# Second layer of a two-layer model in fp32r: expert weights brought to the rows by DMA through DRAM instead of by matmuls

## The chip, the cores and the metric

The kernel runs on one core of a Trainium2 chip. The metric is the device time of one execution in microseconds.

## What is computed

Input x has 4 sequences of 512 rows and 512 columns. Two layers follow each other; in both, x becomes x + s * silu(f), with s and f computed from the normalised rows.

```python
# layer 1: s = masked linear, f = FFN over the argmax of each block of 32
# layer 2:
qkv = xn @ Wqkv + bqkv
attn = softmax(q @ k.T / sqrt(128)); s = (attn @ v) @ Wo + bo
base_out = xn @ base_w.T + base_b
res_hidden = xn @ A.T                      # 64 columns
logits = xn @ router_w.T                   # 16 experts
topw, topi = top_k(softmax(logits), 2); topw /= sum(topw) + 1e-6
combine = sum(one_hot(topi) * topw)        # [row, expert]
delta = einsum('bse,bsr,eor->bso', combine, res_hidden, B)
f = base_out + delta * 0.5
```

The last product is computed as one matrix product over 16 x 64 = 1024 values per row: `prod[e*64 + r, row] = combine[row, e] * res_hidden[row, r]`, eight tiles of 128 partitions.

## The kernel before, in words

Every fp32 product is made of three fp32r matmuls: each operand is split into a rounded part (`_hi`) and the remainder (`_lo`), and `three` (L414) issues hi x hi, hi x lo and lo x hi. ScalarE rounds, VectorE or GpSimd subtract. The five engines run lists that are written out by hand in program order (`chunk` in each engine's block) and are tied together by semaphores; nothing reorders them. Layer 1 (until about 408 us) is not touched by the change but for small things. Between the layers the rows go through DRAM (`mid_state`).

Layer 2 works on one sequence at a time, here called a chunk (0 to 3); chunk 0 is written out, 1 and 2 are a loop, 3 is written out. In TensorE's `chunk` (L1368) the order is: res_hidden and logits (bank `pj[0]`), q, k and v with the transposes of the logits and of the routing weights (`comb`) between them, scores of row tile 0, then scores 1 to 3 with base products (`base`, L1324) and spreading matmuls between them, the transposes of the probabilities (`probs_transpose`, L1350), half of the products with B (`lora`, L1332), the product with v ("pv"), the other halves of lora, the output projections (`project`, L1362), then base and lora of row tiles 2 and 3, with the transposes of the next chunk's normalised rows (`transpose_rows`, L344) around lora of tile 3.

The routing weights of a row must reach all 64 partitions of each expert. Before, the transposed weights lie in `combT` (16 rows, and their remainders in 16 more), and a matmul with the 0/1 matrix `pick`, built once on GpSimd (L620 to L628), spreads them over 128 partitions:

```python
nc.tensor.matmul(pj[kt % 2][:], pick[:, kt, :], combT[:], start=True, stop=True).then_inc(spread_done, 1)
```

This is done for each of the eight tiles kt (`spread`, L1316). VectorE multiplies the bank by `res` (`prods`, L1063), ScalarE rounds the product (`prods_hi`, L799), GpSimd forms the remainder (L672), and lora waits for it (`prod_split`). The product buffer `prod` has three places, so product kt waits for remainder kt - 3.

VectorE's `chunk` (L1119) also holds the maxima of the scores (`score_peak`), the remainders of the transposed probabilities (`probs_lo`, L1070), the bias of y and s and the silu (`y_out`, `s_out`, `silu`), and for the next chunk the statistics, the normalisation (`rows_norm`, L384) and the remainders of its transposed rows (`rows_lo`, L358). The transpose of next rows 2 waits for `xT_done` of next rows 0, as both use one bank. GpSimd gates: after silu it multiplies g by s and adds x_res (`gate`, L391). Of layer 1's last four gates, the second and later ones wait for the second `qk_lo` of chunk 0 (L657).

SyncE issues all DMAs. It ends layer 1 with the four row stores of the last sequence, each after its gate, and the wait for them (L533); in layer 2 (L548) each chunk loads x_res, then x_tile of the next chunk, stores four row tiles, and waits for these stores.

Of the eight banks, `pj` are 0 and 1, `y` 2 and 3, `sc` 4 and 5, `tr` 6 and 7.

## Time and profile before

| what | value |
|---|---|
| median of 3 runs | 650.04 us (650.01 to 650.18) |
| the profiled execution, its own time | 650.05 us |
| its span in the profile | 648.2 us |
| TensorE matmuls busy | 632.3 us, 98% of the span |
| VectorE busy | 446.3 us, 69% |
| GpSimd busy | 240.0 us, 37% |
| ScalarE busy | 213.4 us, 33% |

The span runs from the first to the last instruction of the profiled execution; its own time is 1.85 us longer. Matmuls overlap in the records (one of 512 columns is listed with 0.39 us but the next starts 0.227 us after it), so a stretch is priced by its start and end, not by the sum of its records. Layer 2 begins with the matmul at 407.96 us; the chunks begin some 58.9 us apart.

### The profile page before, as it was taken

The page shows a single profiled execution, that of the slowest core. Times are in us where ns is not written, and L with a number is a line of the kernel's source. Part 1 is how long each engine was busy: PE and PEld are TensorE (multiplying, and loading weights), DVE is VectorE, ACT ScalarE, POOL GpSimd, SP SyncE. Part 2 cuts the span into 40 slices and gives each one's busy share as a digit, 9 for nine tenths or more (in the row PEclk, how much of TensorE's full clock was granted, in tenths as well). Part 3 has the DMA queues.
Part 4 walks back from the last instruction along what each step waited for, and adds up shares of the span by engine and source line. Part 5 has one row for each costly group of instructions (what it writes and reads, how often), then busy time and mean ns, then how long its engine had stood idle before and what let it go on. Part 6 is the DMA issues. An engine that isn't in the chain of part 4 may idle for free.

```text
span 648.2 us, 8466 instructions
## 1 busy us (share of the span) xinstructions
PE 632.3 (98%) x2942; PEld 509.9 (79%) x2942; DVE 446.3 (69%) x716; ACT 213.4 (33%) x379; POOL 240.0 (37%) x188
## 2 busy tenths in 40 slices
PE   7999999999999999999999999999999999999997
PEld 3768787878888878888878787778878878887887
DVE  7987776787765777765777886655765857575633
ACT  3533333312223312223322243651255035314510
POOL 2355545650000740000742644582425433351441
PEclk9999999999999999999999999999999999999999
DMA  9940000022400022300153622050140013012000
GB/s 282 400 158 1 2 0 1 26 81 52 127 17 9 26 81 70 108 16 8 32 141 95 173 82 73 17 178 1 49 147 1 16 50 129 0 41 89 2 32 33
DMA packets 42575, 46.16 MB, mean 71 GB/s; under 512 B 25072, under 2 KB 25456, under 8 KB 41904
## 3 DMA queue, kind: packets, MB, share of 16 engines
q1 hardware_dynamic: 42544, 45.76, 22.1%
q8 instruction: 18, 0.29, 0.2%
q14 instruction: 13, 0.11, 0.1%
HBM read 31.85 MB, written 8.39 MB: 62 GB/s over the span
## 4 chain that ended last, share of the span: by engine, by line
PE 81%; DVE 12%; issue 3%; ACT 1%; POOL 1%; DMA 1%; DVEq 0%; POOLq 0%; ACTq 0%; SPq 0%
PE bank L418 73%; DVE counts L940 3%; PE bank L348 2%; DVE seg_top L926 2%; DVE eq L928 2%; PE bank L1205 1%; PE bank L1359 1%; DMA first<-counts 1%; PE bank L1183 1%; DVE h_lo L970 1%; PE bank L1322 1%; DVE h L961 1%; POOL g_tile L394 1%; PE bank L1224 1%; DVE ws_raw L994 0%
## 5 line engine op out<-in xcount | busy, mean ns | idle before, releaser
L418 PE MATMUL bank<-w_hi_t,h_hi 128*128 128x512 f32 x224 | 90.4, 404 | 0.7 <-DVE h_lo L970 0.4
L761 ACT ACTIVATE h_hi<-h 128x512 fp32r<-128x512 f32 x56 | 35.4, 633 | 162.9 <-DVE h L961 162.9
L418 PE MATMUL bank<-w_lo_t,h_hi 128*128 128x512 f32 x224 | 87.6, 391 | 0.0
L418 PE MATMUL bank<-xT_hi,w_hi_t 128*128 128x512 f32 x224 | 87.4, 390 | 0.1
L418 PE MATMUL bank<-w_hi_t,h_lo 128*128 128x512 f32 x224 | 87.4, 390 | 0.0
L418 PE MATMUL bank<-xT_hi,w_lo_t 128*128 128x512 f32 x224 | 87.2, 389 | 0.0
L418 PE MATMUL bank<-xT_lo,w_hi_t 128*128 128x512 f32 x224 | 87.1, 389 | 0.0
L940 DVE TENSOR_TENSOR_SCAN counts<-restart,eq 128x512 bf16<-128x512 bf16 (+1 forms) x56 | 76.0, 1357 | 2.4
L394 POOL TENSOR_TENSOR g_tile<-g_tile,s_tile 128x512 f32<-128x512 f32 x31 | 44.3, 1430 | 88.3 <-DVE g_tile L983 44.2
L926 DVE TENSOR_REDUCE seg_top<-bank 128x16 f32<-128x512 f32 (+1 forms) x64 | 39.5, 617 | 46.2 <-PE bank L1205 46.2
L672 POOL TENSOR_TENSOR prod_lo<-prod,prod_hi 128x512 fp32r<-128x512 f32 x32 | 40.6, 1291 | 57.9 <-ACT prod_hi L801 57.8
L970 DVE TENSOR_TENSOR h_lo<-h,h_hi 128x512 fp32r<-128x512 f32 x56 | 42.0, 751 | 27.0 <-ACT h_hi L761 25.4
L380 POOL TENSOR_TENSOR rstd<-mean_var,eps 128x4 f32<-128x4 f32 x8 | 1.6, 201 | 159.1 <-DVE mean_var L374 159.1
L740 ACT ACTIVATE h<-bank 128x512 f32<-128x512 f32 x56 | 33.5, 598 | 57.4 <-DVE h_lo L970 47.3
L418 PE MATMUL bank<-b_hi,prod_hi 128*128 128x512 f32 (+1 forms) x136 | 52.1, 383 | 0.0
L418 PE MATMUL bank<-b_hi,prod_lo 128*128 128x512 f32 (+1 forms) x136 | 51.3, 377 | 0.0
L418 PE MATMUL bank<-b_lo,prod_hi 128*128 128x512 f32 (+1 forms) x136 | 51.3, 377 | 0.0
L418 PEld LDWEIGHTS bank<-w_hi_t,h_hi 128*128 128x128 f32 x224 | 42.1, 188 | 10.7 <-DVE h_lo L970 2.3
L418 PEld LDWEIGHTS bank<-w_hi_t,h_lo 128*128 128x128 f32 x224 | 42.1, 188 | 9.4
L418 PEld LDWEIGHTS bank<-xT_hi,w_hi_t 128*128 128x128 f32 x224 | 42.0, 188 | 9.1 <-ACT s_tile L695 0.4
L418 PEld LDWEIGHTS bank<-xT_hi,w_lo_t 128*128 128x128 f32 x224 | 42.0, 188 | 8.7
L418 PEld LDWEIGHTS bank<-xT_lo,w_hi_t 128*128 128x128 f32 x224 | 42.1, 188 | 8.7
(191 smaller groups left out, 1300.5 us busy)
## 6 DMA issues: line engine op xcount, KB each, us to landing
w_raw<-in_w SPq DMA_DIRECT2D x28, 256.0 KB, 10.1
x_res<-in_x SPq DMA_DIRECT2D x4, 1024.0 KB, 8.5
mid_state<-g_tile SPq DMA_DIRECT2D x16, 256.0 KB, 2.1
x_tile<-mid_state SPq DMA_DIRECT2D x4, 1024.0 KB, 7.4
x_res<-mid_state SPq DMA_DIRECT2D x4, 1024.0 KB, 5.5
out<-g_tile SPq DMA_DIRECT2D x15, 256.0 KB, 2.0
x_tile<-in_x SPq DMA_DIRECT2D x3, 1024.0 KB, 5.6
b_raw<-in_lora_b SPq DMA_DIRECT2D x2, 1024.0 KB, 5.1
```

Of the source, the lines that this page charges most:

```text
L348: last = nc.tensor.transpose(rows_bank(g, tt)[:, k * P:(k + 1) * P], x_tile[:, tt, k * P:(k + 1) * P], ident[:])
L394: nc.gpsimd.tensor_tensor(g_tile[:, tt, :], g_tile[:, tt, :], s_tile[:, tt, :], ALU.mult).then_inc(s_free, 1)
L418: last = nc.tensor.matmul(dst, a, b, start=(start and n == 0), stop=(stop and n == len(mms) - 1))
L672: nc.gpsimd.tensor_tensor(prod_lo[:, kt, :], prod[:, kt % 3, :], prod_hi[:, kt, :].bitcast(F32), ALU.subtract).then_inc(prod_split, 1)
L740: nc.scalar.activation(h[:], up[it % 2][:], ACT.Relu).then_inc(relu_done, 1)
L761: nc.scalar.activation(h_hi[:, it % 2, :], h[:], ACT.Copy).then_inc(h_hi_done, 1)
L926: nc.vector.reduce_max(seg_top[:, 0:segs], got, AX.X).then_inc(seg_max, 1)
L928: nc.vector.tensor_tensor(eq[:, 0:PW[p]].rearrange("p (s n) -> p s n", n=SEG), got, seg_top[:, 0:segs, None].to_broadcast([P, segs, SEG]), ...
L940: nc.vector.tensor_tensor_scan(kept[:, tt, 0:PW[p]], restart[:, 0:PW[p]], eq[:, 0:PW[p]], 0.0, ALU.mult, ALU.add).then_inc(sel_count, 1)
L961: nc.vector.scalar_tensor_tensor(h[:], which, 1.0, h[:], ALU.is_equal, ALU.mult).then_inc(h_masked, 1)
L970: nc.vector.tensor_tensor(h_lo[:, it % 2, :], h[:], h_hi[:, it % 2, :].bitcast(F32), ALU.subtract).then_inc(h_split, 1)
L1183: last = nc.tensor.matmul(sel[:], c1_stack[:, k, :], x[:, k, :], start=(k == 0 and x is xT_hi), stop=(k == KD - 1 and x is xT_lo))
```

## The change

The `pick` matrix and the spreading matmuls are gone. ScalarE copies the 16 transposed rows of weights to `combT` (now plain fp32, no remainder), SyncE stores them to DRAM (`expert_weights`, 32 KB), waits for the store, and copies them back with eight DMAs, each of which repeats rows over 64 partitions for two tiles (256 KB). The copies land in `spread`, which shares its place with prod_lo. These nine DMAs stand ahead of the load of x_res. VectorE multiplies `spread` by `res`, both in SBUF.

As banks 0 and 1 are free of spreading, y has four banks (0 to 3), and base of tiles 0 to 2 (and of 3, but in the last chunk) goes ahead of lora. lora waits tile by tile of prod. VectorE takes all score maxima first and the products after them: three before the remainders of the probabilities 0 and 1, the fourth between, four behind. `comb` is written once, without the padding.

```diff
@@ -172,9 +171,10 @@
+        spread = raw_at("spread", [P, KE, S], next_1l.end)
...
-        combT = next_1l.take("combT", [P, S], F32R)
+        combT = next_1l.take("combT", [P, S])
@@ -437,10 +435,12 @@
-        y = [banks[2], banks[3]]
+        y = [banks[tt] for tt in range(TT)]
+        y_end = [banks[3], banks[1]]
+        KG = KE // 4
...
-        NROUTE = 19
+        NROUTE = 18
@@ -547,6 +547,13 @@
+                sp.wait_ge(comb_out, c + 1)
+                sp.dma_start(weights, combT[0:E, :]).then_inc(st_weights, 16)
+                sp.wait_ge(st_weights, c * 16 + 16)
+                for i in range(4):
+                    for j in range(EPT):
+                        sp.dma_start(spread[j * R:(j + 1) * R, i * KG:(i + 1) * KG, :],
+                                     weights_of[j:j + 1, i * KG:(i + 1) * KG, :].to_broadcast([R, KG, S])).then_inc(ld_spread[i], 16)
@@ -820,7 +818,7 @@
-                        nc.scalar.activation(combT[0:2 * Q, :], tr[0][0:2 * Q, :], ACT.Copy).then_inc(comb_hi, 1)
+                        nc.scalar.activation(combT[0:E, :], tr[0][0:E, :], ACT.Copy).then_inc(comb_out, 1)
@@ -829,21 +827,17 @@
-                prods_hi(c, 0)
-                prods_hi(c, 1)
-                probs_exp(c, 1)
-                prods_hi(c, 2)
-                prods_hi(c, 3)
-                probs_exp(c, 2)
-                probs_exp(c, 3)
-                prods_hi(c, 4)
-                prods_hi(c, 5)
+                for tt in range(1, TT):
+                    probs_exp(c, tt)
+                for kt in range(3):
+                    prods_hi(c, kt)
...
+                prods_hi(c, 3)
...
-                prods_hi(c, 6)
-                prods_hi(c, 7)
+                for kt in range(4, KE):
+                    prods_hi(c, kt)
@@ -1062,26 +1053,22 @@
-                dve.wait_ge(spread_done, c * KE + kt + 1)
+                dve.wait_ge(ld_spread[kt // KG], c * EPT * 16 + EPT * 16)
...
-                nc.vector.tensor_tensor(prod[:, kt % 3, :], pj[kt % 2][:], res[:], ALU.mult).then_inc(prod_done, 1)
+                nc.vector.tensor_tensor(prod[:, kt % 3, :], spread[:, kt, :], res[:], ALU.mult).then_inc(prod_done, 1)
...
-            def two_prods(c, kt):
-                prods(c, kt)
-                prods(c, kt + 1)
-
...
-                nc.vector.tensor_tensor(g_tile[:, tt, :], y[tt % 2][:], bias_b[:], ALU.add).then_inc(y_read, 1)
+                nc.vector.tensor_tensor(g_tile[:, tt, :], y[tt][:], bias_b[:], ALU.add).then_inc(y_read, 1)
@@ -1117,32 +1104,26 @@
-                if is_first:
-                    dve.wait_ge(up_done, CH * IT)
-                    nc.vector.memset(combT[2 * Q:P, :].bitcast(F32), 0.0).then_inc(comb_zero, 1)
...
-                dve.wait_ge(comb_hi, c + 1)
-                nc.vector.tensor_tensor(combT[Q:2 * Q, :], tr[0][Q:2 * Q, :], combT[Q:2 * Q, :].bitcast(F32),
-                                        ALU.subtract).then_inc(comb_split, 1)
...
-                two_prods(c, 0)
...
-                score_peak(c, 1)
-                two_prods(c, 2)
-                score_peak(c, 2)
-                score_peak(c, 3)
-                two_prods(c, 4)
+                for tt in range(1, TT):
+                    score_peak(c, tt)
+                for kt in range(3):
+                    prods(c, kt)
...
+                prods(c, 3)
...
-                two_prods(c, 6)
+                for kt in range(4, KE):
+                    prods(c, kt)
@@ -1313,35 +1294,31 @@
-            def spread(c, kt):
-
-                if kt < 2:
-                    pe.wait_ge(proj_read, c * 4 + kt + 1)
-                else:
-                    pe.wait_ge(prod_done, c * KE + kt - 1)
-                nc.tensor.matmul(pj[kt % 2][:], pick[:, kt, :], combT[:], start=True, stop=True).then_inc(spread_done, 1)
-
...
-                    pe.wait_ge(y_read, c * TT + TT + tt - 1)
-                three(y[tt % 2][:], [(xT_hi[:, k, rows(tt)], xT_lo[:, k, rows(tt)], base_hi[:, k, :], base_lo[:, k, :])
+                    pe.wait_ge(y_read, c * TT + tt + 1)
+                    if tt < 2:
+                        pe.wait_ge(proj_read, c * 4 + tt + 1)
+                three(y[tt][:], [(xT_hi[:, k, rows(tt)], xT_lo[:, k, rows(tt)], base_hi[:, k, :], base_lo[:, k, :])
...
-                pe.wait_ge(prod_split, c * KE + k1)
-                last = three(y[tt % 2][:], [(prod_hi[:, k, rows(tt)], prod_lo[:, k, rows(tt)], b_hi[:, k, :], b_lo[:, k, :])
-                                            for k in range(k0, k1)], start=False, stop=(k1 == KE))
+                for k in range(k0, k1):
+                    if tt == 0:
+                        pe.wait_ge(prod_split, c * KE + k + 1)
+                    last = three(y[tt][:], [(prod_hi[:, k, rows(tt)], prod_lo[:, k, rows(tt)], b_hi[:, k, :], b_lo[:, k, :])],
+                                 start=False, stop=(k == KE - 1))
...
-                pe.wait_ge(y_read, c * TT + TT + tt - 1 + i)
-                three(y[1 - i][:, cols],
+                pe.wait_ge(y_read, c * TT + TT + 2 * i)
+                three(y_end[i][:, cols],
@@ -1398,70 +1376,61 @@
-                            combined = nc.tensor.transpose(tr[0][0:2 * Q, rows(tt)], comb[:, tt, :], ident[:])
+                            combined = nc.tensor.transpose(tr[0][0:E, rows(tt)], comb[:, tt, :], ident[:])
...
-                    pe.wait_ge(pick_ready, 4)
...
-
-                if is_first:
-                    pe.wait_ge(comb_zero, 1)
-                pe.wait_ge(comb_split, c + 1)
-                spread(c, 0)
-                spread(c, 1)
...
-                spread(c, 2)
-                spread(c, 3)
...
+                base(c, 1, 0, 2)
...
-                base(c, 1)
-                spread(c, 4)
-                spread(c, 5)
+                base(c, 1, 2, KD)
+                base(c, 2)
...
+                if not last_chunk:
+                    base(c, 3, 0, 2)
+                probs_transpose(c, 2)
+                probs_transpose(c, 3)
+                if not last_chunk:
+                    base(c, 3, 2, KD)
...
-                probs_transpose(c, 2)
-                probs_transpose(c, 3)
-                spread(c, 6)
-                spread(c, 7)
-                lora(c, 1, 0, 4)
...
-                lora(c, 0, 4, 8)
+                lora(c, 0, 4, KE)
...
-                lora(c, 1, 4, 8)
+                lora(c, 1, 0, KE)
...
-                base(c, 2)
-                lora(c, 2, 0, 8)
+                lora(c, 2, 0, KE)
...
-                    base(c, 3)
+                    pe.wait_ge(y_read, c * TT + TT + 2)
...
-                    lora(c, 3, 4, 8)
+                    lora(c, 3, 4, KE)
```

**TensorE, chunk 0, from the last spreading matmuls before the probabilities to the first product with B.** L1359 are the transposes of the probabilities (L1337 in the changed kernel), L1322 the spreading matmuls, L418 (L416) the matmuls of `three`. Before:

```order
L1322 MATMUL bank<-combT,pick 128x512 [waits prod_done] x2
L1359 MATMUL bank<-ident,probs 128x128 [waits exp_done]
L1359 MATMUL bank<-ident,probs 128x128 x3
L1359 MATMUL bank<-ident,probs 128x128 [waits v_split]
L1359 MATMUL bank<-ident,probs 128x128 x3
L418 MATMUL bank<-b_hi,prod_hi 128x512 [waits prod_split,b_split]
```

Now:

```order
L1337 MATMUL bank<-ident,probs 128x128 [waits exp_done,comb_out]
L1337 MATMUL bank<-ident,probs 128x128 x3
L1337 MATMUL bank<-ident,probs 128x128 [waits v_split]
L1337 MATMUL bank<-ident,probs 128x128 x3
L416 MATMUL bank<-base_hi,xT_hi 128x512 [waits y_read]
L416 MATMUL bank<-base_lo,xT_hi 128x512
L416 MATMUL bank<-base_hi,xT_lo 128x512
L416 MATMUL bank<-base_hi,xT_hi 128x512
L416 MATMUL bank<-base_lo,xT_hi 128x512
L416 MATMUL bank<-base_hi,xT_lo 128x512
L1337 MATMUL bank<-ident,probs 128x128 [waits p_split]
L1337 MATMUL bank<-ident,probs 128x128 x3
```

Twelve matmuls of lora stood between the second and the third transpose of the probabilities; now six of base(3) do, and in the last chunk none.

**VectorE, chunk 0, from the last score maximum to the reciprocal of the sums.** Before:

```order
L1059 TENSOR_REDUCE s_max<-bank 128x1 [waits score_done]
L1061 TENSOR_SCALAR s_neg<-s_max 128x1 [waits score_max]
L1068 TENSOR_TENSOR prod<-bank,res 128x512 [waits prod_split,spread_done] x2
L1072 TENSOR_TENSOR pT_lo<-bank,pT_hi 128x512 [waits p_hi_done] x4
L1068 TENSOR_TENSOR prod<-bank,res 128x512 [waits prod_split,spread_done] x2
L1147 RECIPROCAL p_inv<-p_sum 128x4 [waits exp_done]
```

Now:

```order
L1050 TENSOR_REDUCE s_max<-bank 128x1 [waits score_done]
L1052 TENSOR_SCALAR s_neg<-s_max 128x1 [waits score_max]
L1059 TENSOR_TENSOR prod<-spread,res 128x512 [waits ld_spread_0] x2
L1059 TENSOR_TENSOR prod<-spread,res 128x512 [waits ld_spread_1]
L1063 TENSOR_TENSOR pT_lo<-bank,pT_hi 128x512 [waits p_hi_done] x2
L1059 TENSOR_TENSOR prod<-spread,res 128x512 [waits prod_split,ld_spread_1]
L1063 TENSOR_TENSOR pT_lo<-bank,pT_hi 128x512 [waits p_hi_done] x2
L1059 TENSOR_TENSOR prod<-spread,res 128x512 [waits prod_split,ld_spread_2] x2
L1059 TENSOR_TENSOR prod<-spread,res 128x512 [waits prod_split,ld_spread_3] x2
L1128 RECIPROCAL p_inv<-p_sum 128x4 [waits exp_done]
```

The remainder pT_lo 0 now stands behind products 0 to 2, the third of which waits for the second pair of copies; five products stand behind pT_lo 1, where two stood behind pT_lo 3.

**SyncE, from the last row stores of layer 1 into layer 2's first chunk.** Before:

```order
L486 DMA mid_state<-g_tile 128x512 [waits rows_done] x4
L567 UNCONDITIONAL_BRANCH [waits st_rows]
L567 ISA
L550 DMA x_res<-mid_state 128x4x512
L552 ISA
```

Now:

```order
L486 DMA mid_state<-g_tile 128x512 [waits rows_done] x4
L574 UNCONDITIONAL_BRANCH [waits st_rows]
L574 ISA
L551 DMA expert_weights<-combT 16x512 [waits comb_out]
L552 ISA
L555 DMA spread<-expert_weights 64x2x512 [waits st_weights]
L555 DMA spread<-expert_weights 64x2x512 x7
L557 ISA
L557 DMA x_res<-mid_state 128x4x512
```

The store of the weights and the eight copies stand where x_res was loaded, behind the wait for layer 1's stores.

## Rows read from the trace of the kernel before

**Rows 1.** The page, part 4: the chain that ended last, by engine.

```profile
PE 81%; DVE 12%; issue 3%; ACT 1%; POOL 1%; DMA 1%; DVEq 0%; POOLq 0%; ACTq 0%; SPq 0%
```

**Rows 2.** Waits, whole span: waiting line <- releaser, us in total, times, longest.

```profile
PE bank L348 <- DVE x_tile L388: 2.4, 2, 1.9
...
PE bank L1359 <- ACT probs L796: 1.4, 1, 1.4
```

**Rows 3.** The chain in order of time, chunk 1: start us, us, what.

```profile
479.85 0.44 PE bank L1401 x4
...
495.49 0.47 PE bank L1322 x2
495.96 23.81 PE bank L418 x105
519.77 0.88 PE bank L348 x8
```

**Rows 4.** Timeline of VectorE, chunk 0: start, length, line, [idle before <- releaser].

```profile
428.73 0.69 DVE L1068 TENSOR_TENSOR prod<-bank,res 128x512 f32<-128x512 f32 x1 [2.28 <-POOL prod_lo L672]
...
433.39 1.29 DVE L1072 TENSOR_TENSOR pT_lo<-bank,pT_hi 128x512 fp32r<-128x512 f32 x2 [1.18 <-ACT pT_hi L805]
```

**Rows 5.** Timeline of SyncE's queue, end of layer 1 and chunks 0 and 1.

```profile
427.40 0.33 SPq L486 DMA_DIRECT2D mid_state<-g_tile  x1
429.70 0.41 SPq L550 DMA_DIRECT2D x_res<-mid_state  x1
430.39 0.40 SPq L553 DMA_DIRECT2D x_tile<-mid_state  x1
...
476.15 0.41 SPq L550 DMA_DIRECT2D x_res<-mid_state  x1
```

**Rows 6.** The page, part 6: DMA issues, KB each, median us to landing.

```profile
x_tile<-mid_state SPq DMA_DIRECT2D x4, 1024.0 KB, 7.4
...
b_raw<-in_lora_b SPq DMA_DIRECT2D x2, 1024.0 KB, 5.1
...
bias_a<-in_bo SPq DMA_DIRECT2D x1, 256.0 KB, 8.5
...
out<-g_tile SPq DMA_DIRECT2D x2, 128.0 KB, 1.7
```

**Rows 7.** Timeline of ScalarE, chunk 0: rounding of the probabilities 0 and 1.

```profile
432.78 1.06 ACT L805 ACTIVATE pT_hi<-bank 128x512 fp32r<-128x512 f32 x2
```

**Rows 8.** Timeline of TensorE, chunk 0: the transposes of comb.

```profile
419.16 0.60 PE L1401 MATMUL bank<-ident,comb 128*64 128x128 f32 x4
```

**Rows 9.** Timeline of SyncE's queue: 2 MB of loads and a row repeated over 128 partitions.

```profile
350.95 0.38 SPq L497 DMA_DIRECT2D x_tile<-mid_state  x1
...
351.93 0.49 SPq L513 DMA_DIRECT2D bias_a<-in_bo  x1
```

**Rows 10.** Timeline of GpSimd, chunk 1: two remainders of products.

```profile
487.72 2.55 POOL L672 TENSOR_TENSOR prod_lo<-prod,prod_hi 128x512 fp32r<-128x512 f32 x2 [0.59 <-ACT prod_hi L801]
```

**Rows 11.** Timeline of VectorE in layer 1: an instruction with two SBUF inputs.

```profile
361.69 1.50 DVE L970 TENSOR_TENSOR h_lo<-h,h_hi 128x512 fp32r<-128x512 f32 x1 [0.70 <-ACT h_hi L761]
```

**Rows 12.** Timeline of GpSimd beside it.

```profile
361.48 2.73 POOL L625 TENSOR_SCALAR_AFFINE_SELECT pick_raw<-pick_raw 128x1024 f32<-128x1024 f32 x2
```

**Rows 13.** Timeline of VectorE, chunk 1: y of tile 1 to silu of tile 2.

```profile
508.82 0.69 DVE L1084 TENSOR_TENSOR g_tile<-bank,bias_b 128x512 f32<-128x512 f32 x1
...
512.60 5.81 DVE L388 TENSOR_SCALAR x_tile<-x_tile,mean_var,rstd 128x512 f32<-128x512 f32 x4 [1.41 <-POOL rstd L382]
...
519.71 0.69 DVE L1098 SCALAR_TENSOR_TENSOR g_tile<-probs,g_tile 128x512 f32<-128x512 f32 x1
```

**Rows 14.** Line 388, the normalisation: ns min/median/max.

```profile
L388 DVE TENSOR_SCALAR x_tile<-x_tile,mean_var,rstd x32: 541/544/1516, 10.5 to 575.8; 128x512 f32<-128x512 f32 x32
```

**Rows 15.** Timeline of TensorE, the program's start: the stretches from 0 and from 5 us.

```profile
1.66 7.66 PE L1276 MATMUL bank<-restart 128*128 128x512 bf16 x28 [1.66 <-DVE restart L872]
...
4.62 1.68 PE L1276 MATMUL bank<-restart 128*128 128x512 bf16 x7
```

More of the change, by code:

```diff
@@ L138, in block_mask_ffn_then_attention_lora_kernel @@
         c1_nat = span_c.take("c1_nat", [P, KD, RANK])
[L139 to L143 removed]
+        span_s = Span(phase(span_c.end))
         ws_hi = span_s.take("ws_hi", [P, KD, D], F32R)
```

37 lines of the change are left out of this document (11 added, 26 removed).

## The prediction, made before the changed kernel ran

> **What bounds the kernel now.** I read the page's busy shares first: TensorE's matmuls are busy 98% of the span (part 1, in the table above), and the chain that ended last is 81% TensorE (part 4) [rows 1]. Then the waits: TensorE's longest is 1.9 us, for the normalised rows at the start, and in the second layer, where the change is, it waits once, 1.4 us, before the transposes of the probabilities [rows 2]. The chain in order of time shows chunk 1 as an unbroken run of TensorE work [rows 3]: 105 matmuls in 23.81 us, so one costs 0.227 us of TensorE's time, eight transposes 0.87, two spreading matmuls 0.45 to 0.47. A matmul removed there is worth its full time, and a wait put there costs its full time. The question is how late each helper becomes.
>
> **What goes.** Eight spreading matmuls per chunk, four pairs at 0.46 us, four chunks: **-7.4 us** [rows 3]. The 1.4 us wait in chunk 0 goes too: there the score maxima stood behind a product that waited for GpSimd (2.28 us [rows 4]); now all maxima come first on VectorE: **-1.4 us**. The 4.7 us of `pick` building on GpSimd, the remainder of combT on VectorE (0.68), one of two writes of comb and the memset lie beside TensorE work: nothing.
>
> **Chunk 0's copies are late.** SP runs its list in order. The DMAs of the weights now stand where x_res was loaded, and SP came there only at 429.70, after the last row store of layer 1, which waits for its gate and left at 427.40 [rows 5]. Nothing in the change moves that, as the gates wait for qk_lo, not for `pick`. The small store: that row store let SP go on 2.3 us later; the smallest store shown takes 1.7 us to land [rows 6]. I take 2.3, so the copies start at 432.0. Product 2 needs four of the eight, 1 MB together: a load of 1 MB lands in 5.1 us [rows 6], and I add 0.2 for four issues: 437.3. Then product 2 (0.69), its rounding (0.6, as another bank of that size), and behind it in the same queues pT_hi 0 (0.6) and pT_lo 0 (0.69) [rows 4, 7], with some 0.05 between engines: 440.1. TensorE's third transpose of probabilities waits for that. It arrives after 57 matmuls and 12 transposes from 419.6 (the end of the transposes of comb [rows 8]): 12.9 + 1.3 = 14.2, at 433.8. **Stall 6.4 us**, rounded up; lowest, with 1.7 and 5.1, 5.6. For the upper end: a 256 KB copy that repeats one DRAM row, issued at 351.93 behind 2 MB issued from 350.95, landed 8.5 us later, 9.5 from the first issue, where 2 MB without it take 8.1 (issued 429.70 and 430.39, the second landing in 7.4) [rows 5, 6, 9]. So repeated rows may take 1.4 us per 256 KB rather than 0.75: 2.6 us more, a stall of 9.0. I take 6.4; plain loads of 2 KB pieces are the nearest. In later chunks SP waits for comb (x_res left at 476.15, comb was transposed at 479.9 [rows 3, 5]); there the copies of product 2 land some 8.4 us after comb (0.6 combT, 2.3 store, 5.3 copies, gaps), before VectorE reaches it at 10.2 (scores 3 at 8.1, their maximum 0.8, two products 1.3), and x_res and x_tile behind them at about 18, needed at 27: hidden, and at the slow rate (22) as well.
>
> **The products come late (every chunk).** Count from the end of comb's transposes. TensorE is at the first probability transposes at 12.0, the second pair at 14.25, and at the last lora tile of row tile 0 at 24.0 (51 + 6 matmuls, 16 transposes, then 6 + 12 + 12 + 9 matmuls). The helpers: pT_lo 1 at 14.6, product 3 behind it 15.2, rounded 15.9, then pT_hi 2 and 3 (1.1) 17.0, pT_lo 3 17.8, product 4 18.4, rounded 19.1, and four remainders on GpSimd at 1.27 [rows 4, 7, 10]: 24.2. That is 0.2 late. Five products now stand behind pT_lo 1, where two did behind pT_lo 3. Moreover a product now has both inputs in SBUF. A VectorE instruction of that kind and size took 1.50 us beside a busy GpSimd, where products that read a bank take 0.69 [rows 4, 11, 12]. Products 6 and 7 run beside the remainders; of their 2 x 0.8 us more, the product buffer hides most and perhaps 0.5 reaches the end of the chain; I take **0.5 us in each of three chunks, 1.5** (0.2 to 0.9). The Trainium skill, "SBUF — State Buffer", section "SBUF: two separate sides", says that VectorE with two SBUF inputs and GpSimd reading SBUF take one shared port pair in turn, each for its whole instruction. By this rule the wait would be 0.7 a chunk, without it 0.2; my 0.5 comes from the row. In the **last chunk** there is no base(3), 12 matmuls or 2.7 us of cover less: TensorE would be there at 21.3 and the remainder at 24.2 to 24.6: **3.1 us** (2.9 to 3.6).
>
> **The next rows come late (chunks 0 to 2).** Base products moved ahead leave only 42 matmuls (project 1, lora 2, project 2, half of lora 3) and eight transposes, 9.5 + 0.9 = 10.4 us, between the end of lora 1 and the third transpose of the next rows, where 66 stood. That transpose waits for xT_lo 0, and VectorE does before it: y, s and silu of tile 1, moments, four normalisations, y, s and silu of tile 2. In the trace this takes from 508.82 to 520.40, then 0.6 to 0.7 for xT_lo: 12.2 us, and it starts 0.2 after lora 1 [rows 13]. The four normalisations are 5.81 us of it, beside GpSimd's gates; half of all take 0.54 each [rows 13, 14]. The gates still come at that time. So 12.4 - 10.4 = 2.0, and 0.2 more for the pair: **2.2 us in each of three chunks, 6.6** (1.8 to 2.2).
>
> **The clock.** TensorE's longest wait in the trace is 1.9 us [rows 2], so no row shows what 6.4 us do. At the program's start, after 1.66 us without work, 28 matmuls of 512 columns took 7.27 us from the first start to the last (7.66 less one record of 0.39), while those from 4.62 us on stand 0.215 us apart ((1.68 - 0.39)/6), which makes 5.8 for 27 [rows 15]. So **1.5 us** were lost before 4.62, half of those 3.0 us: the level of 1.2 GHz instead of 2.4, though the page's granted clock reads 9 or more tenths there. I count that once; bounds 0 and 3.0 (twice as long). The Trainium skill, "TensorE: Matmul & The Clock Gate", section "Why this matters for your kernels", warns that idle gaps between bursts of matmuls bring the engine back to half rate; the trace of before has no gap long enough to show it.
>
> **Sum.** -7.4 - 1.4 + 6.4 + 1.5 + 3.1 + 6.6 + 1.5 = +10.3 us. The profiled execution took 650.05 (span 648.2 and 1.8 around it), the median is 650.04: **660.4 us**. With all lower bounds 655.7 (5.6 + 0.6 + 2.9 + 5.4 + 0 - 8.8), with all upper ones 666.1 (9.0 + 2.7 + 3.6 + 6.6 + 3.0 - 8.8).
>
> **Rivals.**
> - *The clock stays at 2.4 GHz.* For it: it held through all waits of up to 2 us. Against it: the start. 658.9 us. Chance 0.25.
> - *The repeated rows come slowly.* Sixteen engines read the same 2 KB rows and each copy writes half the partitions. For it: the bias load [rows 9]. 2.6 us more in chunk 0 alone: 663.0. Chance 0.13. (The Trainium skill, "SBUF — State Buffer", section "Door 1: The DMA port swizzle", says that 64 neighbouring partitions reach half of the ports that DMA writes through; no transfer of the trace of before has that shape.)
> - *VectorE keeps up, faster.* If the way from y of tile 1 to xT_lo 0 is 10.2 us or less instead of 12.4 (normalisations at 0.54 would save 3.6), and the same engine's products come 3 us sooner in the last chunk, only chunk 0's stall is left: 650.05 - 8.8 + 6.4 = 647.7 with the clock kept, 649.2 without. For it: VectorE loses two instructions per chunk. Against it: both chains are sums of rows of this trace, and the gates that stretch the normalisations are not moved. Chance 0.07.
> - *Only the normalisations are short*: GpSimd's gates stand elsewhere after the shifts, and the 6.6 us at the next rows vanish alone: 653.8. Against it: a gate needs silu, which comes before the normalisations as now. Chance 0.05.
>
> **How the numbers follow.** The forecast has 0.50 at 660.4. The range 655.5 to 665.0 takes in the kept clock and the slow rows and leaves out the faster case, the 653.8 and the sum of all upper bounds (0.12 and a little). A measurement of this kernel can tell about 0.2%, 1.3 us. Faster 0.05 (most of the rival), same 0.02, slower 0.93.
>
> **What would show it.** In the changed profile: SP issues the weights store at 429.7 and the first copy near 432; TensorE idles 6 to 7 us in chunk 0 before a transpose of the probabilities, released by pT_lo; matmuls just behind it stand 0.42 us apart for about 3 us; in chunks 0 to 2 TensorE waits about 2 us for xT_lo before the third transpose of the next rows; before the last lora tile it waits up to 0.7 us for prod_lo, in the last chunk about 3 us in several pieces, the first before a transpose. Chunks 1 and 2 take 59 to 60 us against 58.9. I am wrong if VectorE's four normalisations take about 2 us, or if product 2 runs before 435 in chunk 0.

## The result and the profile after

The changed kernel takes 666.35 us (median of 6 runs, 664.94 to 669.27), the kernel before 650.02 (649.12 to 651.43): a ratio of 1.0264 with a 95% interval of 1.0253 to 1.0276. The forecast was 660.4 with a range up to 665.0: the direction was right, the loss is 16.3 us where 10.3 were forecast, outside the range. The profiled execution took 666.52 us (span 664.7).

The page of the changed kernel, busy times and granted clock (before: TensorE 98% of the span, clock 9 tenths or more throughout), and its chain by engine, which answers to [rows 1]:

```profile
PE 634.4 (95%) x2910; PEld 507.1 (76%) x2910; DVE 449.1 (68%) x706; ACT 213.1 (32%) x379; POOL 238.8 (36%) x184
...
PEclk9999999999999999999999999969899999999999
...
PE 55%; issue 20%; DVE 12%; POOL 9%; ACT 2%; DMA 1%; POOLq 0%; DVEq 0%; ACTq 0%; SPq 0%
```

TensorE issues 32 matmuls fewer, as counted, and is busy 2 us longer, although it also stands more. Part of that is the clock row: matmuls at the lower clock add 5.6 us (worked out below). The rest, some 4 us, stands around the waits: from start to start of the matmuls they cost more than the idle time that is listed. TensorE's waits in layer 2, 405 to 665 us (they answer to [rows 2], where there was one of 1.4 us):

```profile
PE bank L1337 <- DVE pT_lo L1063: 8.7, 2, 7.7
PE bank L346 <- DVE xT_lo L360: 5.8, 3, 2.0
PE bank L416 <- POOL prod_lo L670: 1.8, 5, 0.7
```

All three waits that the forecast named are there, in their places. The copies of chunks 1 to 3 are hidden, as forecast: VectorE waits for copies only twice, 8.8 us in all, both times in chunk 0.

The lengths of the chunks, from the first matmul of one to that of the next (for the last, to its last matmul), show what each cost:

| | chunk 0 | chunk 1 | chunk 2 | chunk 3 |
|---|---|---|---|---|
| before | 60.64 | 58.91 | 58.93 | 57.79 |
| before less 1.85 (8 matmuls) and, in chunk 0, 1.4 | 57.39 | 57.06 | 57.08 | 55.94 |
| changed kernel | 71.10 | 60.49 | 62.10 | 59.68 |
| lost | 13.7 | 3.4 | 5.0 | 3.7 |
| forecast as lost | 10.6 | 2.7 | 2.7 | 3.1 |

The four losses add up to 25.9 us (to 25.8 as rounded in the table), forecast were 19.1: 6.8 us are missing from the forecast. Chunks 1 and 2 do the same work and have the same waits, yet differ by 1.6 us. The windows (stretch, length, PE busy, granted clock, DMA share, GB/s) tell them apart:

```profile
432.00:436.00 4.00, 1.44 (x7) 0.92 0.90 240
436.00:440.00 4.00, 0.00 (x0) 0.50 1.05 244
440.00:444.00 4.00, 2.84 (x11) 0.50 1.05 326
444.00:448.00 4.00, 4.00 (x15) 0.80 0.61 239
...
474.00:476.00 2.00, 2.00 (x6) 0.50 0.30 118
...
536.00:538.00 2.00, 2.00 (x10) 1.00 0.31 120
...
596.00:598.00 2.00, 2.00 (x7) 0.50 0.08 24
```

The first four rows are the stall of chunk 0. The clock falls to 0.50 (1.2 GHz instead of 2.4) while TensorE still stands, some 2 us into the stall, and stays there for a while after it: in the fourth row 15 matmuls stand in 4 us where there would be 18. The other three stand just behind the wait for xT_lo in chunks 0, 1 and 2: after 1.9 us without work the clock is at 0.50, after 2.0 at 1.00, after 2.0 at 0.50 again. The matmuls of the slow stretches start 0.43 us after one another, where 0.23 is usual. Added up, 2.2 us were lost behind the stall, 1.8 behind the wait of chunk 0, some 1.6 in chunk 2: **5.6 us, where the forecast had 1.5**.

Chunk 0 on SyncE, VectorE and TensorE (start, length, line, idle time before and its releaser):

```profile
429.06 0.34 SPq L551 DMA_DIRECT2D expert_weights<-combT  x1
430.66 5.24 SPq L555 DMA_DIRECT2D spread<-expert_weights  x8
```

```profile
435.99 1.30 DVE L1059 TENSOR_TENSOR prod<-spread,res 128x512 f32<-128x512 f32 x2 [7.96 <-DMA spread<-expert_weights]
438.12 1.11 DVE L1059 TENSOR_TENSOR prod<-spread,res 128x512 f32<-128x512 f32 x1 [0.84 <-DMA spread<-expert_weights]
440.41 1.29 DVE L1063 TENSOR_TENSOR pT_lo<-bank,pT_hi 128x512 fp32r<-128x512 f32 x2 [1.18 <-ACT pT_hi L803]
...
463.93 5.78 DVE L386 TENSOR_SCALAR x_tile<-x_tile,mean_var,rstd 128x512 f32<-128x512 f32 x4 [1.41 <-POOL rstd L380]
469.63 0.68 DVE L1071 TENSOR_TENSOR g_tile<-bank,bias_b 128x512 f32<-128x512 f32 x1
470.23 0.74 DVE L1079 SCALAR_TENSOR_TENSOR s_tile<-bank,p_inv,bias_a 128x512 f32<-128x512 f32 x1
471.00 0.69 DVE L1085 SCALAR_TENSOR_TENSOR g_tile<-probs,g_tile 128x512 f32<-128x512 f32 x1
471.61 1.28 DVE L360 TENSOR_TENSOR xT_lo<-bank,xT_hi 128x512 fp32r<-128x512 f32 x2
```

```profile
441.16 1.97 PE L1337 MATMUL bank<-ident,probs 128*128 128x128 f32 x8 [7.72 <-DVE pT_lo L1063]
...
472.35 1.71 PE L346 MATMUL bank<-ident,x_tile 128*128 128x128 f32 x8 [1.89 <-DVE xT_lo L360]
```

Store and wait took 1.6 us instead of 2.3, the copies began 1.3 sooner than forecast; but product 2 started 7.46 us after the first copy's issue instead of 5.3, and the stall is 7.7 us instead of 6.4. Product 2 itself took 1.11 us instead of 0.69, as it ran beside GpSimd's first remainder. The second group shows the normalisations at 5.78 us as in [rows 13] and xT_lo behind y, s and silu of tile 2.

### The profile page after: what moved, and what is told of

The parts are those of the page before. It is cut to its first block, busy times and chain, and to the rows that moved or that the text cites. A ratio compares the mean times of both kernels' runs of the same rounds, so it can differ in the third digit from the quotient of the medians.

```text
span 664.7 us, 8426 instructions
## 1 busy us (share of the span) xinstructions
PE 634.4 (95%) x2910; PEld 507.1 (76%) x2910; DVE 449.1 (68%) x706; ACT 213.1 (32%) x379; POOL 238.8 (36%) x184
## 4 chain that ended last, share of the span: by engine, by line
PE 55%; issue 20%; DVE 12%; POOL 9%; ACT 2%; DMA 1%; POOLq 0%; DVEq 0%; ACTq 0%; SPq 0%
PE bank L416 51%; POOL prod_lo L670 5%; DVE counts L933 3%; POOL g_tile L392 2%; DVE seg_top L919 2%; DVE eq L921 2%; PE bank L346 1%; PE bank L1186 1%; POOL g_tile L396 1%; DMA first<-counts 1%; DVE x_tile L386 1%; PE bank L1164 1%; DVE h_lo L963 1%; DVE h L954 1%; PE bank L1205 1%
## 5 line engine op out<-in xcount | busy, mean ns | idle before, releaser
L416 PE MATMUL bank<-w_hi_t,h_hi 128*128 128x512 f32 x224 | 90.3, 403 | 0.3
L416 PE MATMUL bank<-w_lo_t,h_hi 128*128 128x512 f32 x224 | 87.6, 391 | 0.0
L416 PE MATMUL bank<-xT_hi,w_hi_t 128*128 128x512 f32 x224 | 87.4, 390 | 0.1
L416 PE MATMUL bank<-w_hi_t,h_lo 128*128 128x512 f32 x224 | 87.4, 390 | 0.0
L416 PE MATMUL bank<-xT_hi,w_lo_t 128*128 128x512 f32 x224 | 87.2, 389 | 0.0
L416 PE MATMUL bank<-xT_lo,w_hi_t 128*128 128x512 f32 x224 | 87.2, 389 | 0.0
L670 POOL TENSOR_TENSOR prod_lo<-prod,prod_hi 128x512 fp32r<-128x512 f32 x32 | 44.5, 1416 | 76.8 <-ACT prod_hi L799 76.8
L416 PE MATMUL bank<-b_hi,prod_hi 128*128 128x512 f32 (+1 forms) x136 | 54.2, 398 | 2.0 <-POOL prod_lo L670 1.8
L416 PE MATMUL bank<-b_lo,prod_hi 128*128 128x512 f32 (+1 forms) x136 | 52.3, 385 | 0.0
L416 PE MATMUL bank<-b_hi,prod_lo 128*128 128x512 f32 (+1 forms) x136 | 52.2, 384 | 0.0
L416 PEld LDWEIGHTS bank<-w_hi_t,h_hi 128*128 128x128 f32 x224 | 42.1, 188 | 10.0 <-DVE h_lo L963 1.5
L416 PEld LDWEIGHTS bank<-w_hi_t,h_lo 128*128 128x128 f32 x224 | 42.1, 188 | 9.4
L416 PEld LDWEIGHTS bank<-xT_hi,w_hi_t 128*128 128x128 f32 x224 | 42.0, 188 | 9.1 <-ACT s_tile L693 0.4
L416 PEld LDWEIGHTS bank<-xT_hi,w_lo_t 128*128 128x128 f32 x224 | 42.1, 188 | 8.8
L416 PEld LDWEIGHTS bank<-xT_lo,w_hi_t 128*128 128x128 f32 x224 | 42.1, 188 | 8.6
```

The lines of the kernel that those rows point to most:

```text
L416: last = nc.tensor.matmul(dst, a, b, start=(start and n == 0), stop=(stop and n == len(mms) - 1))
L670: nc.gpsimd.tensor_tensor(prod_lo[:, kt, :], prod[:, kt % 3, :], prod_hi[:, kt, :].bitcast(F32), ALU.subtract).then_inc(prod_split, 1)
```

## The experiments

Each is compared with runs of the kernel before on the same chip (medians 649.75 to 650.11 us). Lengths of chunks and clocks are read from one profiled execution each. Its time differs from the median by up to 2.4 us, so what an edit is worth is taken from the medians, and the profiles say where.

**The price of the clock.** If the clock falls because TensorE stands, then work without purpose must make the kernel faster. Filling the long stall (the helper `fill` is written out here):

```
+                if is_first:
+                    for _ in range(32):
+                        nc.tensor.matmul(sc[1][:], base_hi[:, 0, 0:P], base_hi[:, 0, :], start=True, stop=True)
                 probs_transpose(c, 2)
```

> The changed kernel, with 32 matmuls on TensorE (512 columns, into a bank nobody reads) put before the third transpose of the probabilities of chunk 0, where TensorE stands 7.7 us. They shorten no wait of VectorE or of a DMA, they only keep TensorE busy (32 x 0.215 = 6.9 us). Theory A, the clock: the matmuls behind the stall ran 0.43 us apart until 445.5 because the granted clock fell to 0.50, which cost 2.2 us; with TensorE kept busy they run at 0.22 and the time is 666.35 - 2.2 = 664.1 us, at most 664.9 if a wait for prod_lo that the slow matmuls covered comes out (0.7). Theory B, the matmuls there are slow for another reason (the copies into SBUF run beside them): the time stays at 666.3 or rises by the little that the filling overshoots. Granted clock of 436 to 448: A 1.00, B about 0.5.

Measured: 663.68 us (ratio 1.0209, 1.0195 to 1.0223), 2.7 us faster with 32 matmuls more. Granted clock 1.00 in every window from 428 to 452; theory B falls, as the copies ran at the same rate beside it. In its profiled execution (665.25 us, mean clock 0.992) the clock fell behind the waits for xT_lo of chunks 0 and 1 (0.50 at 472 and at 534) and not behind that of chunk 2; its other four runs are 1.1 to 2.8 us shorter at 0.996 to 0.997. After the same wait it falls sometimes.

It fell a third time in that execution, in layer 1, behind the very wait that [rows 2] shows with 1.9 us and behind which the clock had stayed up. The code there is the same. That wait and the window behind it, in the kernel before and in this one:

```profile
11.24 1.50 PE L348 MATMUL bank<-ident,x_tile 128*128 128x128 f32 x12 [1.92 <-DVE x_tile L388]
12.00:13.00 1.00, 0.74 (x7) 1.00 0.96 375
```

```profile
11.23 2.15 PE L346 MATMUL bank<-ident,x_tile 128*128 128x128 f32 x9 [2.04 <-DVE x_tile L386]
12.00:13.00 1.00, 1.00 (x7) 0.50 1.06 203
```

Layer 2 begins at 407.40 us all the same (407.35 in the changed kernel), so the fall costs nothing visible there. In the profiles of all runs together, TensorE has 18 waits of 1.89 to 2.04 us, and the clock fell behind 11 of them; it fell behind none of the 18 waits of 0.96 to 1.75 us. Why it falls behind one wait and not behind another of the same length stays open here.

```
                     lora(c, 3, 0, 4)
+                    for _ in range(8):
+                        nc.tensor.matmul(tr[1][:], base_hi[:, 0, 0:P], base_hi[:, 0, :], start=True, stop=True)
                     for tt in (2, 3):
```

> As the run before, and 8 more such matmuls (1.7 us) before the third transpose of the next rows in chunks 0, 1 and 2, where TensorE waits 1.9 to 2.0 us for xT_lo. Theory A, the clock is also lost behind waits of 2 us: a further 1.8 us in chunk 0 and 1.5 in chunk 2 come back (the granted clock read 0.50 there), nothing in chunk 1: 664.1 - 3.3 = 660.8 us, to 661.6 with the wait for prod_lo. Theory B, those waits cost only themselves, and the clock falls only behind the long stall: 664.1, as with the first filling alone. If A holds, the clock cost 5.5 us of the change's 16.3.

Measured: 662.39 us (1.0196, 1.0182 to 1.0209), clock 1.00 throughout layer 2: 4.0 us less than the changed kernel. It is only 1.3 less than the first filling and not 3.3, a step that the intervals of the two runs don't separate. In the other executions of the first filling the clock falls about once each, by their mean of 0.996 to 0.997 (three falls made 0.992), where this forecast counted on two. Chunk 0 shows in part why the whole isn't 5.6: it takes 68.46 us, 2.6 less and not 4.0, since with the clock up the wait for prod_lo comes out that slow matmuls had covered. The clock thus costs 5.6 us as slow matmuls and 4.0 us of the kernel's time.

**The copies behind the row stores.**

```
                     store_row(c, place, tt)
+                    if tt == 0 and not to_next:
+                        spread_rows(0)    # wait for combT, store, wait, eight copies
```

> The changed kernel, with SyncE's work for chunk 0's weights (wait for combT, store, wait, eight copies) taken from behind the last row store of layer 1 to a place behind its first row store; nothing else moves. combT is written by 419.75, so the copies should start near 421.5 and product 2 find its four copies landed near 429. Theory A, SyncE's place in its list makes the stall of 7.7 us: the stall goes and the fall of the clock behind it (2.2 us) with it, less up to 0.7 us of waits for prod_lo that come out: 656.4 to 657.2 us. Rival, the products and their rounding are late anyway in VectorE's queue, whose maxima come first: TensorE would still wait at the third transpose, as much as 2 us, and the time would be 658 to 660. Second rival, the row stores of layer 1, now behind the copies, make the load of x_res or of the next rows late: a wait of GpSimd's or VectorE's in the list that is not there now.

Measured: 657.14 us (1.0119, 1.0103 to 1.0134), 9.2 us less, as theory A has it (the profiled execution took 654.75). Its SyncE queue issues the store at 418.80 and the copies from 420.39; TensorE's third transpose of the probabilities in chunk 0 starts without a wait, the chunk takes 60.47 us instead of 71.10. Neither rival shows: TensorE has no wait for pT_lo in chunk 0, and x_res and x_tile are issued at 433.81 and 434.25, with nothing in chunk 0 waiting for them.

**xT_lo ahead of y, s and silu.**

```
                         rows_norm(dve, c + CH + 1)
+                        for t in range(2):
+                            rows_lo(dve, c + CH + 1, t)
...
-                        for t in range(TT):
+                        for t in (2, 3):
                             rows_lo(dve, c + CH + 1, t)
```

> The changed kernel, with VectorE's xT_lo 0 and 1 of the next rows put behind the normalisations and before y, s and silu of row tile 2 (ScalarE's xT_hi 0 and 1 before the tanh of tile 2 accordingly). Theory A, VectorE's order makes the waits of 1.9 to 2.0 us for xT_lo in three chunks: xT_lo 0 comes 2.0 us sooner, all three waits go (5.8 us) and with them the fall of the clock behind two of them (3.3 us): 657.2 us. Rival, the wait only moves: y, s and silu of tile 2 come 1.3 us later, xT_lo 2 and 3 with them, and TensorE waits at the start of the next chunk, 0.5 to 1.3 us each time: 659 to 661. The stall of chunk 0 stays at 7.7 us in both.

Measured: 656.66 us (1.0107, 1.0091 to 1.0122), 9.7 us less, as theory A has it. VectorE in chunk 0:

```profile
463.18 5.78 DVE L386 TENSOR_SCALAR x_tile<-x_tile,mean_var,rstd 128x512 f32<-128x512 f32 x4 [1.41 <-POOL rstd L380]
468.88 1.27 DVE L360 TENSOR_TENSOR xT_lo<-bank,xT_hi 128x512 fp32r<-128x512 f32 x2
```

xT_lo comes straight behind the normalisations, the waits for it are gone from TensorE's list, chunks 1 and 2 take 58.5 us both and the clock stays at 1.00 there. The loss was an order of instructions, not VectorE's load.

> The changed kernel with both repairs: the copies of chunk 0 behind layer 1's first row store, and xT_lo 0 and 1 ahead of y, s and silu of tile 2. Alone they brought 9.2 and 9.7 us against 666.35. If the two losses are separate, they add: 666.35 - 18.9 = 647.4 us, 0.4% below the kernel before, what is left of the change's gain (8.8 us) after the waits for prod_lo. Rival: they share a part (each gives back clock that the other loses anyway), and the sum is 649 to 651.

Measured: 648.80 us (12 runs; 0.998, 0.9972 to 0.9989), just faster than before and between the two forecasts. The two repairs share 1.4 us of the 18.9: in chunk 0 the first alone brings 10.6 us, the second 3.5, both 12.6. The profiles fit the rival's reason: with either repair alone the clock no longer falls behind the wait for xT_lo of chunk 0 (with the first the wait is there and the clock stays up, with the second the wait is gone), so both count the same fall of the clock, 1.8 us. The clock reads 1.00 throughout layer 2. The kernel now has lost 8 us against a chunk without waits: 58.5 us for 57.06 in three chunks, 59.66 for 55.94 in the last.

**Why copies are slow.**

```
-                                     weights_of[j:j + 1, i * KG:(i + 1) * KG, :].to_broadcast([R, KG, S]))
+                                     mid_rows[0][j * R:(j + 1) * R, (i % 2) * KG:(i % 2 + 1) * KG, :])
```

> The changed kernel, whose eight copies read 64 different rows of 2 KB of another DRAM tensor instead of one row 64 times; sizes, destinations (64 partitions), number and place are the same. The routing weights are therefore wrong, which changes the layer's values only. In the changed kernel the copies move 235 to 255 GB/s with the DMA engines full, while the plain loads behind them move 404 to 408. Theory A, the repeated row is slow: the rate rises to about 400 GB/s, the first four copies land near 5 us instead of 7.4, the stall of chunk 0 shrinks by 2 to 2.5 us and the run takes about 664. Theory B, the half of the partitions is slow: rate and stall stay, 666.

```
-                        sp.dma_start(spread[j * R:(j + 1) * R, i * KG:(i + 1) * KG, :],
-                                     weights_of[j:j + 1, i * KG:(i + 1) * KG, :].to_broadcast([R, KG, S]))
+                        sp.dma_start(spread[:, i * KG + j:i * KG + j + 1, :],
+                                     weights_of[0:1, i * KG + j:i * KG + j + 1, :].to_broadcast([P, 1, S]))
```

> The changed kernel, whose eight copies each write one product's block on all 128 partitions, repeating one row of 2 KB 128 times, instead of two blocks on 64 partitions; bytes and number are the same. Both halves get the weights of expert 0's row, which changes the layer's values only. Theory A, the repeated row is slow: the copies stay at about 240 GB/s and the time at 666. Theory B, the half of the partitions is slow: 400 GB/s, four copies in about 5 us, stall shorter by 2 to 2.5 us, 664.

Windows of the changed kernel, of the one with distinct rows and of the one on all partitions, while the copies run (last columns: DMA share, GB/s):

```profile
436.00:438.00 2.00, 0.00 (x0) 0.50 1.04 245
438.00:440.00 2.00, 0.00 (x0) 0.50 1.06 243
...
442.00:444.00 2.00, 2.00 (x9) 0.50 1.05 405
```

```profile
434.00:436.00 2.00, 0.00 (x0) 1.00 1.08 246
436.00:438.00 2.00, 0.00 (x0) 0.85 1.05 236
```

```profile
436.00:438.00 2.00, 0.00 (x0) 0.83 0.52 198
438.00:440.00 2.00, 0.64 (x3) 0.50 0.64 219
```

And of the changed kernel at its start, while loads of 256 KB onto 128 partitions run (`w_raw`, rows of 2 KB that don't repeat):

```profile
20.00:24.00 4.00, 4.00 (x19) 1.00 1.05 406
```

With different rows (665.17 us, one run) the rate stays, as theory B has it: the DMA engines are full at some 240 GB/s, where the plain loads on 128 partitions behind the copies make 405 at the same share. Product 2 starts 7.1 us after the first issue instead of 7.46. So the repeated row is not the cause of full engines. Nor is the size of a copy, as loads of 256 KB onto 128 partitions make 406. What is left is that a copy writes 64 partitions; eight copies of different rows onto 128 partitions in this place, which would show it directly, were not run. On all 128 partitions (664.71 us, one run) the engines are only busy to 0.5 to 0.7, TensorE's stall is 6.3 us, and product 2 starts 5.7 us after the first issue instead of 7.46; but the rate isn't 400 either. Neither theory forecast engines that stand partly idle. A row repeated over 128 partitions thus meets another limit, near 200 to 260 GB/s in this one run, that doesn't keep the engines busy; which one, no run here shows. The Trainium skill, "SBUF — State Buffer", section "Door 1: The DMA port swizzle", has 64 neighbouring partitions reach half of the ports that DMA writes through; the 240 against 405 GB/s agree roughly (half of 405 is 203).

**The maxima alone.** The forecast gave the change 1.4 us for them.

```
                 score_peak(c, 1)
-                two_prods(c, 2)
+                if not is_first:
+                    two_prods(c, 2)
                 score_peak(c, 2)
                 score_peak(c, 3)
+                if is_first:
+                    two_prods(c, 2)
```

> The kernel before, with one thing of the change: in chunk 0 the maxima and the exponentials of the scores come ahead of products 2 and 3 on VectorE and ScalarE. The forecast priced this part at 1.4 us, the wait of TensorE before the transposes of the probabilities: 650.0 - 1.4 = 648.6. Rival: products 2 and 3 come later by two maxima, so the spreading matmuls 4 and 5 wait for their banks and the gain is 0 to 1.

Measured: 649.90 us (1.0000, 0.9989 to 1.0011), no gain. The one wait of layer 2 only has another name:

```profile
PE bank L418 <- POOL prod_lo L672: 1.1, 1, 1.1
```

The rival has the gain right, 0 to 1, but not the reason. GpSimd comes to the remainders at 427.40, behind layer 1's gates, as before (427.34), so TensorE, let go at the probabilities, waits a little later for prod_lo. In the changed kernel the 1.4 us are gone: with the copies early, chunk 0 is as long as chunk 2 (60.47 and 60.45 us). That this is so because base products stand ahead of lora there is argued from the lists; no run takes them away alone.

**The remainders.** What costs 1.4 us a chunk with both repairs, where the trace lists a wait of 0.28?

```
-                for kt in range(3):
+                for kt in range(4):
                     prods(c, kt)
                 probs_lo(c, 0)
                 probs_lo(c, 1)
-                prods(c, 3)
+                prods(c, 4)
+                prods(c, 5)
                 probs_lo(c, 2)
                 probs_lo(c, 3)
-                for kt in range(4, KE):
+                for kt in range(6, KE):
```

> Both repairs, and the products in another order on VectorE: product 3 ahead of pT_lo 0 (where VectorE stands idle), products 4 and 5 between pT_lo 1 and pT_lo 2, then 6 and 7; on ScalarE the roundings follow. With both repairs a chunk takes 58.5 us, where 58.91 less the spreading matmuls (1.85) make 57.06: 1.4 us too much in each of three chunks, and 3.7 in the last. Theory A: that is GpSimd's chain of remainders. It stands idle 1.4 and 1.8 us in the middle of the eight because products 3 and 4 come late, and then does four in 5.8 us, the last ending at 502.95, when TensorE is at that tile of lora since 501.7. With products 3 to 5 sooner the last remainder ends 2.4 us sooner: 648.8 - 3 x 1.4 - 2.4 = 642.2 us. Rival: the products ahead of pT_lo make pT_lo 0 or 2 late, and TensorE waits 0.5 to 1.0 us for it at the third transpose of the probabilities in each chunk: 645 to 647.

> As the run before, and two more places where TensorE gets work instead of a wait: in the last chunk the base part of the left half of the last row tile (12 matmuls of 256 columns, 1.3 us) goes between the second and third transpose of the probabilities, where it waits 0.98 us for pT_lo 0; and in every chunk the first projection goes ahead of the last two tiles of lora of row tile 0 (0.7 us more cover for prod_lo). Theory A: 642.2 - 1.0 - up to 0.3 = 641.0 us, 1.4% below the kernel before. Rival: the half matmuls cost more than their columns, or the projection waits for the attention's remainder (at_lo comes 2 us behind the product of v) and the wait only changes its place: 642 to 643.

Measured: 646.05 us (0.9931, 0.9918 to 0.9945) and 645.95 (0.994, 0.9926 to 0.9953). The first comes out as its rival has it (645 to 647), by pT_lo; the second misses both of its forecasts (641.0, and 642 to 643) and is no faster than the first. GpSimd and VectorE of the first, chunk 1:

```profile
488.47 12.70 POOL L678 TENSOR_TENSOR prod_lo<-prod,prod_hi 128x512 fp32r<-128x512 f32 x8 [17.77 <-ACT prod_hi L807]
```

```profile
490.01 1.75 DVE L1071 TENSOR_TENSOR prod<-spread,res 128x512 f32<-128x512 f32 x1 [1.18 <-POOL prod_lo L678]
491.69 1.28 DVE L1075 TENSOR_TENSOR pT_lo<-bank,pT_hi 128x512 fp32r<-128x512 f32 x2
492.88 2.38 DVE L1071 TENSOR_TENSOR prod<-spread,res 128x512 f32<-128x512 f32 x2
```

The waits for prod_lo are gone, as theory A has it, but each engine now slows the other: a product takes 1.75 or 1.2 us instead of 0.68, a remainder 1.59 instead of 1.29, while pT_lo, which reads a bank, stays at 0.64 to 0.69 between them. pT_lo comes later: chunks 0 to 2 take 57.9 us instead of 57.1, and in the last TensorE waits 1.4 and 0.8 us for it. In the second kernel the filling of the last chunk pays (57.73 us instead of 58.92), but with the projection moved ahead chunks 0 to 2 take 58.3 instead of 57.9: in chunk 1 it starts 0.22 us late and the matmul behind it another 0.11; what makes up the rest of the 0.4 stays open.

> Both repairs, and of the other order of products only product 4 moved: behind product 3, between pT_lo 1 and pT_lo 2, where VectorE stands idle 1.2 us; product 3 stays behind pT_lo 1. In the run with products 3 to 5 sooner GpSimd's remainders ran without a gap (12.70 us for eight, 1.59 each against 1.27 alone) and every product beside them took 1.2 to 1.75 us against 0.63 to 0.69, so pT_lo 0 and 2 came later and TensorE waited 0.8 us a chunk for them. Theory A, the port shared by VectorE with two SBUF inputs and GpSimd: a product in a gap of GpSimd takes 0.7 us and delays nothing; the last remainder ends 1.4 us sooner, a chunk takes 57.1 us instead of 58.5, and the time is 648.8 - 3 x 1.4 - 1.2 = 643.4 us. Rival: product 4 is stretched as well and makes pT_lo 2 late, or the remainders stretch so that the last one ends little sooner: 57.7 or more a chunk, 645.5 or more.

> As the run before, and in the last chunk the base part of the left half of the last row tile (12 matmuls of 256 columns) between the second and third transpose of the probabilities, where TensorE waits 0.98 us for pT_lo 0. In the run with all repairs this made the last chunk 57.73 us instead of 58.92. Theory A: 643.4 - 1.2 = 642.2 us, 1.2% below the kernel before. Rival: with product 4 sooner little is left to cover, 643.

The first moves product 4 alone (`prods(c, 4)` behind `prods(c, 3)`, which stays where it was); the second adds, in TensorE's list:

```
+                else:
+                    end_base(c)    # base part of the left half of the last tile, into y_end[0]
                 probs_transpose(c, 2)
```

Measured: 645.85 us (0.9931, 0.9917 to 0.9946) and **644.40 us (0.9913, 0.9899 to 0.9928)**, the fastest kernel of the study, 0.9% below the one before. Neither reaches theory A's time (643.4 and 642.2): the first lies where its rival has it (645.5 or more). Chunks take 57.8 us: one product moved gives all that three gave (57.9), but not the 57.1 expected. In the first, chunk 1 on VectorE and GpSimd:

```profile
492.01 1.28 DVE L1070 TENSOR_TENSOR prod<-spread,res 128x512 f32<-128x512 f32 x2
...
495.08 2.89 DVE L1070 TENSOR_TENSOR prod<-spread,res 128x512 f32<-128x512 f32 x3
```

```profile
497.51 4.12 POOL L678 TENSOR_TENSOR prod_lo<-prod,prod_hi 128x512 fp32r<-128x512 f32 x3 [1.29 <-ACT prod_hi L807]
```

Products 3 and 4 take 1.28 us together, so product 4 is not stretched. But the last three products (2.89 us) and remainders (4.12) still slow each other, and the last remainder ends 0.7 us sooner within its chunk than with both repairs, not 1.4. From start to start the trace shows two small rests in chunk 1, 0.27 us at the last lora tile and about as much at the third transpose of the next rows. The filling of the last chunk brings 1.4 us between the two medians, where 1.2 were forecast.

## Why the forecast was right in sign and wrong in size

- *What goes, -7.4:* right as far as shown. With both repairs and product 4 moved, the clock is at 1.00 and the arithmetic of 57.06 us a chunk is approached to 0.7, of which two small waits explain 0.5.
- *-1.4 for the maxima:* right in the sum, but not by that edit alone, which brings nothing.
- *Chunk 0's stall, 6.4:* right in its mechanism, mis-sized; 7.7 idle, 8.0 from start to start. Store and wait 1.6 for 2.3, copies 7.46 for 5.3 us. The forecast took "plain loads of 2 KB pieces are the nearest", which write 128 partitions; these copies write 64. The rival of slow copies was nearer: it gave them 2.6 us more, measured were 2.2 more. Of its two reasons the half of the partitions fits the runs, the repeated row doesn't.
- *The products, 1.5 in three chunks:* too low per chunk. The two waits of chunk 1 cost 0.39 and 0.56 us from start to start, 0.95, where I took 0.5; in chunk 0 slow matmuls covered them. The shared port is there: products 0.68 alone and up to 1.76 beside a remainder. The products of the kernel before, with one input in a bank, and of the changed one, with both in SBUF (ns min/median/max):

```profile
L1068 DVE TENSOR_TENSOR prod<-bank,res x32: 681/682/694, 422.6 to 615.4; 128x512 f32<-128x512 f32 x32
```

```profile
L1059 DVE TENSOR_TENSOR prod<-spread,res x32: 681/684/1761, 436.0 to 633.4; 128x512 f32<-128x512 f32 x32
```

  The Trainium skill, "SBUF — State Buffer", section "SBUF: two separate sides", lets VectorE with two SBUF inputs and GpSimd lock each other out for a whole instruction; the trace agrees in that each is slowed by the other (the 12.70 us row, 1.59 us a remainder, and products of up to 1.76 us), and the 0.7 that the forecast gave for the rule would have been nearer than my 0.5.
- *Last chunk, 3.1:* 3.7 lost.
- *The next rows, 6.6:* right: 1.89, 1.98 and 1.98 us idle, some 0.2 more each from start to start.
- *The clock, 1.5:* this is **the step that failed**. "I count that once" was wrong: it fell three times in the profiled execution and cost 5.6 us. I took the 1.9 us wait of [rows 2], behind which the clock had stayed up, as proof that such waits are harmless, and did not ask again for the three waits of 2.2 us that the forecast itself adds. The runs show that it falls behind some waits of 1.9 to 2.0 us and not behind others, in other executions behind that same wait of layer 1 too: one trace in which it stayed up proved nothing. The Trainium skill, "TensorE: Matmul & The Clock Gate", section "Why this matters for your kernels", warns only of idle gaps longer than these; here gaps of 1.9 us were enough.

The measured 666.35 us lie above even the forecast's sum of all upper bounds, 666.1, and the clock is the one term that lies far outside its own bounds: 5.6 us (4.0 by the fillings), where the forecast had 0 to 3.0. The stall (8.0 in 5.6 to 9.0), the products (1.9 in 0.6 to 2.7) and the next rows (6.6, at the upper end of 5.4 to 6.6) lie within theirs, the last chunk 0.1 above. But it isn't alone. The kernel with both fillings, whose clock stays up, takes 662.4 us, where the forecast has 658.9 with the clock kept: 3.5 us of the 6.0 that the forecast was short belong to the stall and the late products, 2.5 to the clock (4.0 for 1.5). The products count more by this reckoning, as slow matmuls no longer cover them in chunk 0. Neither sign of being wrong that the forecast named came (the normalisations took 5.78 us, product 2 ran at 438.12); of its other signs, chunks 1 and 2 of 59 to 60 us didn't, they took 60.5 and 62.1.

In the profiled execution's own terms, of the missing 6.8 us the clock is 4.1, the stall 1.6, the last chunk 0.6 and the remainders of chunks 0 to 2 0.4. With what was measured, 8.0 for the stall, 5.6 for the clock, 1.9 and 3.7 for the products and 6.6 for the rows, the sum is 25.8 - 8.8 = 17.0; the span grew by 16.5, as layer 1 ended 0.6 us sooner in that execution (407.35 against 407.96). Chunk by chunk the pieces fit less well than in the sum: 14.2 for 13.7 in chunk 0, 3.2 for 3.4 and 4.8 for 5.0 in chunks 1 and 2.

## What to carry to other kernels

Before a change that takes work off a full TensorE, list what each helper has to deliver and when: removing 32 matmuls was worth 7.4 us, and three late helpers took 26 back, of which moving instructions within the lists recovered 22 (666.35 to 644.40). Price a wait on TensorE as the wait plus a possible fall of the clock behind it, every time it occurs, and read waits from start to start of the matmuls, as the idle column shows less than is lost. When a DMA takes an engine's place, look where its issue stands in its queue's list, and how many partitions it writes.

## What the runs showed that was not expected

- The clock fell behind waits of only 1.9 to 2.0 us, and not every time: in the changed kernel's profile behind those of chunks 0 and 2, with the first filling behind those of 0 and 1 and behind the 2.0 us wait of layer 1; in all profiles together behind 11 of 18. Matmuls without purpose in the waits brought 4.0 us.
- Copies onto 64 partitions: 235 to 250 GB/s with full DMA engines, whether one row is repeated or not; loads onto 128 make 405. A row repeated over 128 partitions: some 200 to 260 GB/s with engines busy to 0.5 to 0.7, in one run.
- A store to DRAM of 32 KB and the wait for it held SyncE's list 1.6 us.
